# First attention: sums closed in four column groups, reciprocals widened by copies, one multiply

## The chip, the cores and the metric

The kernel runs on one core of one Trainium2 chip. A core has five engines that work side by side and wait for each other through semaphores: TensorE (PE in the profile, its weight loads PEld), VectorE (DVE), ScalarE (ACT), GpSimd (POOL) and SyncE (SP), which issues DMAs. The metric is the time of one execution on the device in microseconds, lower is better. The time before is 1979.07 us, the median of 3 runs (1977.02 to 1979.21).

## The reference

Four layers follow each other, each an attention and a feed-forward block on 2048 tokens of width 128. Only the first attention is touched. It has 16 query heads and 4 key heads of width 64, two sequences of 1024 tokens, and a causal mask:

```python
q = (x @ Wq + bq).reshape(b, s, NQ, D)
k = (x @ Wk + bk).reshape(b, s, NKV, D)
v = (x @ Wv + bv).reshape(b, s, NKV, D)
q = _rotary(q)
k = _rotary(k)
...
logits = jnp.einsum('bqhgd,bkhd->bhgqk', qg, k) * scale
logits = jnp.where(causal, logits, jnp.float32(-1e+30))
w = jax.nn.softmax(logits, axis=-1)
out = jnp.einsum('bhgqk,bkhd->bqhgd', w, v).reshape(b, s, NQ * D)
return out @ Wo + bo
```

The change concerns the division inside `softmax`: each weighted sum of values is divided by the sum of its row's exponentials.

## The kernel before

**Tiling.** An attention works through 16 head pairs (`j` in `attention_order`: 2 sequences times 8 pairs), and each pair through two chunks of 512 queries, c = 0 and c = 1. For a chunk, TensorE computes scores transposed, keys on the partitions and queries in the free dimension: one key tile of 128 keys, two heads, up to 512 queries each (`score`, written S below; 4 key tiles for c = 0 and 8 for c = 1). The two heads' scores go to PSUM banks P0 and P1, always these two, and ScalarE takes the exponentials from there into an SBUF tile `pr` (L1440, or L1435 for narrow tiles). The next S can only write P0 when the exponential has read it. GpSimd masks diagonal tiles (L1667) and adds the tiles up in `acc` (L1686, L1689). TensorE multiplies `pr` with the values (`pv`, written V), head 0 in PSUM partitions 0 to 63, head 1 in 64 to 127. Before the scores of a chunk, TensorE and VectorE find row maxima (`max`, written M; VectorE L2094, L2105) from other banks, TensorE transposes them (`rows`, written R, L993) and ScalarE negates them (L1418).

**Closing a chunk.** `close` (C) multiplies `acc` with a matrix of ones, which leaves the sum of exponentials of head 0 in partitions 0 to 63 of a bank and that of head 1 in 64 to 127, over 512 columns. Each such multiply is in fp32 and shows as two records, so that a close of the first attention is 4 records. ScalarE then makes a first reciprocal as exp(-ln(sum)) into `rd` (`yinv`, L1459 and L1461). VectorE improves it with one Newton step in two instructions (L2169, L2170) and multiplies the weighted values with it into `z` (L2176). These three are one item, `div` (D). After every second pair, `out` (O) multiplies `z` with the output weights (16 matmuls) and VectorE adds the result to `sacc`.

**What sets the order.** One list of items, made in `attention_order`, is walked by every engine's program; each engine issues its own instructions of each item in the order of the list and waits on semaphores. Nothing is reordered at run time. The string `STEPS[0]` spells the items of one pair: S, M, V, C, D, R, O as above, `q` and `k` projections for the next pair, `v` values, `+` one item of other work (layer norms, the router, its dispatch copies L1492 and GpSimd's gathers L1697). The digit of C, D and O is the distance back: C1, D1 close and divide the second chunk of the pair before (c = 1) while this pair begins, C0 and D0 the first chunk of this pair (c = 0) once its four tiles are added up. PSUM banks 4, 5, 6 and 2 rotate between close, projections, maxima, rows and out. The bank of a close is held from its item to its `div`.

The third attention (after 1430 us) already closes its chunks in four column groups of 32 columns, except the last pair, and takes another way for the reciprocal (a DMA to fold and to spread it). The second attention closes as the first.

## Time and profile before

| | |
|---|---|
| median of 3 runs | 1979.07 us |
| profiled execution | 1971.85 us, of which span 1970.1 us |
| PE busy | 1823.4 us, 93% of the span |
| DVE busy | 1348.2 us, 68% |
| POOL busy | 1203.3 us, 61% |
| ACT busy | 940.0 us, 48% |
| granted TensorE clock, mean | 0.975 |
| first attention | about 40 to 536 us |
| first feed-forward | about 536 to 657 us |

Busy is the union of the instructions' times on an engine. Matmuls overlap in the records, since one starts while the one before still drains, so what a matmul costs TensorE is better read from the distance between starts. The views used below are the page, the table of stretches (busy time of each engine between two times), the chain of waits (the work that ended last, followed back), the timeline of one engine and the groups of instructions by shape.

### The profile page before, as it was taken

How to read it: one execution, taken by the hardware profiler on the slowest of the kernel's cores; microseconds unless marked ns; L12 is line 12 of the kernel's file. 1: busy time of each engine (PE TensorE's matmuls, PEld its weight loads, DVE VectorE, ACT ScalarE, POOL GpSimd, SP SyncE). 2: the span in 40 equal slices, each digit the busy share in tenths (PEclk: the TensorE clock that was granted, in tenths of full speed). 3: DMA queues.
4: the chain of work that ended last, by engine and by line, in shares of the span. 5: the costliest groups of instructions: out<-in, count | busy, mean ns of one | idle time of the engine just before them, and what ended most of it. 6: DMA issues, size and time to landing. Idle time of an engine off the chain costs nothing.

```text
span 1970.1 us, 31876 instructions
## 1 busy us (share of the span) xinstructions
PE 1823.4 (93%) x10080; PEld 1264.4 (64%) x10080; DVE 1348.2 (68%) x3795; ACT 940.0 (48%) x1978; POOL 1203.3 (61%) x1424
## 2 busy tenths in 40 slices
PE   5999999999896799999999999999789999989985
PEld 4566666666595566766766667787556666655564
DVE  8888888888344867666666546547677787776633
ACT  2544445445455454555555434545334444444443
POOL 1766788889654457777777720011266676689853
PEclk8999999999998899999999999999889999999998
DMA  5224243232163433434434220000312223223243
GB/s 152 68 66 113 65 107 91 61 81 62 37 192 84 99 91 87 105 90 102 103 79 115 66 89 22 1 13 1 81 44 69 64 62 88 63 73 85 71 128 96
DMA packets 138568, 155.96 MB, mean 79 GB/s; under 512 B 34480, under 2 KB 78800, under 8 KB 138144
## 3 DMA queue, kind: packets, MB, share of 16 engines
q1 hardware_dynamic: 134304, 145.80, 30.3%
q0 software_dynamic: 4096, 8.12, 1.3%
q8 instruction: 81, 1.33, 0.3%
q14 instruction: 87, 0.71, 0.1%
HBM read 47.96 MB, written 17.52 MB: 33 GB/s over the span
## 4 chain that ended last, share of the span: by engine, by line
PE 59%; DVE 13%; POOL 11%; issue 6%; DMA 4%; ACT 3%; SPq 3%; POOLq 0%; DVEq 0%; ACTq 0%
PE P L894 58%; POOL acc L1689 4%; POOL yd L1706 3%; DVE P L2105 2%; DVE mx L2094 2%; POOL xg L1697 2%; SPq L1810 2%; DMA qA<-hq 1%; POOL acc L1686 1%; POOL pr L1667 1%; ACT pr L1440 1%; PE P L993 1%; DMA rb<-sum_share 1%; DVE mx L2115 1%; DVE mx L2105 0%
## 5 line engine op out<-in xcount | busy, mean ns | idle before, releaser
L1689 POOL TENSOR_TENSOR acc<-acc,pr 128x512 f32<-128x512 f32 (+5 forms) x640 | 659.3, 1049 | 42.8 <-ACT pr L1440 17.0
L1440 ACT ACTIVATE pr<-P 128x512 f32<-128x512 f32 (+1 forms) x768 | 396.4, 568 | 359.0 <-PE P L894 318.9
L894 PE MATMUL P<-pr,vt 128*64 128x512 f32 (+3 forms) x2304 | 403.2, 490 | 4.0 <-POOL pr L1667 4.0
L894 PE MATMUL P<-qA,kA 128*128 128x512 f32 (+2 forms) x1024 | 387.5, 382 | 9.5 <-ACT pr L1440 8.8
L894 PE MATMUL P<-qB,kB 128*128 128x512 f32 (+2 forms) x1024 | 366.2, 363 | 0.0
L894 PE MATMUL P<-kA,qA 128*128 128x512 f32 (+2 forms) x1152 | 314.6, 375 | 36.7 <-DMA qA<-hq 11.9
L1667 POOL TENSOR_SCALAR_AFFINE_SELECT pr<-pr 128x256 f32<-128x256 f32 x384 | 156.7, 409 | 314.1 <-ACT pr L1440 243.8
L894 PEld LDWEIGHTS P<-pr,vt 128*64 128x64 f32 x2304 | 154.5, 137 | 223.8 <-issue 190.3
L2094 DVE TENSOR_REDUCE mx<-P 128x1 f32<-128x512 f32 x384 | 243.1, 684 | 36.0 <-PE P L894 34.1
L894 PEld LDWEIGHTS P<-kA,qA 128*128 128x128 f32 x1152 | 192.1, 195 | 107.1 <-issue 25.2
L894 PEld LDWEIGHTS P<-qA,kA 128*128 128x128 f32 x1024 | 194.1, 190 | 85.8 <-ACT pr L1440 41.3
L1686 POOL TENSOR_TENSOR acc<-pr,pr 128x512 f32<-128x512 f32 (+3 forms) x160 | 213.5, 1343 | 58.2 <-ACT pr L1440 58.0
L2105 DVE CUSTOM_DVE_ANT_0 P<-P,maskQ 128x128 f32<-128x128 f32 (+3 forms) x384 | 177.7, 523 | 59.7 <-PE P L894 57.9
L894 PEld LDWEIGHTS P<-qB,kB 128*128 128x128 f32 x1024 | 194.3, 190 | 21.4
L2105 DVE CUSTOM_DVE_ANT_0 P<-P,maskQ,mx 128x384 f32<-128x384 f32 (+3 forms) x384 | 191.4, 556 | 16.6 <-PE P L894 15.2
L1435 ACT ACTIVATE pr<-P 128x512 f32<-128x512 f32 x192 | 86.9, 488 | 101.8 <-PE P L894 87.2
L2169 DVE SCALAR_TENSOR_TENSOR P<-P,rd 128x512 f32<-128x512 f32 x66 | 46.1, 698 | 122.4 <-ACT rd L1461 122.3
L894 PE MATMUL P<-xh,weights 128*128 128x512 f32 (+1 forms) x336 | 110.4, 411 | 5.9 <-DVE mx L2105 2.1
L1706 POOL DMA_INDIRECT yd<-y,ni x64 | 64.2, 1004 | 78.3 <-DVE y L2400 63.2
L2105 DVE DVE_READ_ACCUMULATOR2_ANT mx<- 128x1 f32 x768 | 109.9, 143 | 0.0
L894 PEld LDWEIGHTS P<-wo,z 128*128 128x128 f32 x768 | 93.4, 194 | 6.9 <-issue 3.1
L894 PE MATMUL P<-wo,z 128*128 128x128 f32 x768 | 96.2, 279 | 1.4 <-DVE z L2176 0.9
(354 smaller groups left out, 2696.6 us busy)
## 6 DMA issues: line engine op xcount, KB each, us to landing
qA<-hq SPq DMA_DIRECT2D x384, 128.0 KB, 2.4
kA<-stage SPq DMA_DIRECT2D x158, 128.0 KB, 2.4
qB<-qB SPq DMA_DIRECT2D x96, 128.0 KB, 2.3
kB<-stage SPq DMA_DIRECT2D x79, 128.0 KB, 2.4
rb<-sum_share SPq DMA_DIRECT2D x60, 128.0 KB, 2.9
yd<-in_c_zero SPq DMA_DIRECT2D x32, 128.0 KB, 2.7
w<-in_L_W SPq DMA_DIRECT2D x16, 256.0 KB, 5.0
xg<-xg SPq DMA_DIRECT2D x24, 129.0 KB
```

What stands on the lines that cost most here:

```text
L894: return P.matmul(out, lhs, rhs, start=start, stop=stop)
L1435: S.activation(a.pr[slot][:, :, 512 - wide:512], src, AF.Exp, scale=0.125).then_inc(s.free[b], 1)
L1440: S.activation(a.pr[slot][:, r, 512 - wide:512], m.bank[b][:, 512 - wide:512], AF.Exp, scale=0.125).then_inc(s.free[b], 1)
L1667: G.affine_select(tile, tile, [[0, 2], [1, 128]], ALU.is_ge, 0.0, 0, -1).then_inc(s.sel, 1)
L1686: G.tensor_tensor(acc[:, :, sl], p0[:, :, sl], pt[:, :, sl], ALU.add).then_inc(s.acc, 1)
L1689: G.tensor_tensor(acc[:, :, sl], acc[:, :, sl], pt[:, :, sl], ALU.add).then_inc(s.acc, 1)
L1697: G.indirect_dma_start(xgd[L], bass.IndirectOffsetOnAxis(ap=r.sidx[:, i // 2, i % 2:i % 2 + 1], axis=0), r.xs[i % 2][:], None).then_inc(s. ...
L1706: G.indirect_dma_start(yd[L], bass.IndirectOffsetOnAxis(ap=e.ni[u % 4][0:wide, t:t + 1], axis=0), e.y[u % 4][0:wide, t, :], None).then_inc ...
L1810: Y.dma_start(a.qA[slot][rows, r, :], hq[64 * r:64 * r + 64, :]).then_inc(s.q_dup[slot], 16)
L2094: V.reduce_max(mx[:, 8 + j:9 + j], ps[:, 0:wide], X).then_inc(s.free[b], 1)
L2105: top = V.tensor_tensor_reduce(tile, tile, m.maskQ[:, 512 - wide:512], 1.0, least, ALU.add, ALU.max, mx[:, j:j + 1])
L2169: chain(V.scalar_tensor_tensor(out=m.bank[b][:], in0=m.bank[b][:], scalar=-1.0, in1=y[:], op0=ALU.mult, op1=ALU.mult))
```

## The change

For the first attention only, a close becomes four multiplies with a ones matrix of 32 columns over 256 query columns each: partitions 0 to 31 hold head 0's queries 0 to 255, 32 to 63 head 0's queries 256 to 511, 64 to 95 and 96 to 127 the same of head 1. ScalarE's two instructions and VectorE's Newton step then run over 256 columns. `div` is split in three items:

- `newt` (N), VectorE: the Newton step over 256 columns; it frees the close's bank.
- `widen` (Y), ScalarE: eight copies of 32 partitions by 256 columns, from `rd` to `z`, two for each group, so that `z` holds the reciprocal in the layout of the weighted values.
- `div` (D), VectorE: one multiply of the weighted values with `z`, in place.

In `STEPS[0]` the sequence "C1 k0\" q1' q0\" D1 q1\" V1 k1 + S M2" becomes "C1 k0\" N1 q1' q0\" q1\" Y1 V1 k1 + S D1 M2", and "D0 R0 M6 S + M5 O0 M8 S" becomes "N0 R0 Y0 M6 S + M5 D0 M8 S O0". The wait of `yinv` for the division before it goes.

```diff
@@ -145,7 +145,7 @@
-                    self.held[b] = (HELD[kind],) + item[1:]
+                    self.held[b] = ("newt" if kind == "close" and item[1] == 0 else HELD[kind],) + item[1:]
@@ -191,6 +191,11 @@
+def quarters(L, b, p):
+
+    return L == 0 or not at_once(L, b, p)
@@ -201,10 +206,10 @@
-    0: ("k0 S q0 k0' R1 S q1 q0' S S C1 k0\" q1' q0\" D1 q1\" V1 k1 + S M2 S M0 k1' S v1 M4 + S M1 C0 V + k1\" + D0 R0 M6 S + M5 O0 M8 S v0 O1 M3 S S M7 V2 + + M9"),
+    0: ("k0 S q0 k0' R1 S q1 q0' S S C1 k0\" N1 q1' q0\" q1\" Y1 V1 k1 + S D1 M2 S M0 k1' S v1 M4 + S M1 C0 V + k1\" + N0 R0 Y0 M6 S + M5 D0 M8 S O0 v0 O1 M3 S S M7 V2 + + M9"),
@@ -1044,7 +1052,7 @@
-                if at_once(*k[0:3]):
+                if not quarters(*k[0:3]):
                     for r in range(2):
                         t = mm(ps[64 * r:64 * r + 64, :], m.ones[:], acc[:, r, :], True, True)
                 else:
...
@@ -1452,13 +1460,25 @@
-                own.mark(S.activation(a.rd[:], m.bank[b][:], AF.Ln))
+                cols = slice(0, 256 if quarters(L, bb, p) else 512)
+                own.mark(S.activation(a.rd[:, cols], m.bank[b][:, cols], AF.Ln))
                 own.settle()
-                S.activation(a.rd[:], a.rd[:], AF.Exp, scale=-1.0).then_inc(s.inv, 1)
+                S.activation(a.rd[:, cols], a.rd[:, cols], AF.Exp, scale=-1.0).then_inc(s.inv, 1)
+            elif kind == "widen":
+                a, old = m.A[k[0]], pl.put_out(*k)
+                z = a.z[pl.chunk(*k) % 4]
+                w.wait_ge(*pl.emptied("close", *k))
+                if old:
+                    w.wait_ge(*pl.filled("out", *old))
+                for g in range(4):
+                    for half in range(2):
+                        rows, cols = 64 * (g // 2) + 32 * half, 256 * (g % 2)
+                        t = S.copy(z[rows:rows + 32, cols:cols + 256], a.rd[32 * g:32 * g + 32, 0:256])
+                t.then_inc(s.widen, 1)
@@ -2161,19 +2181,41 @@
+            elif kind == "newt":
+                y = m.A[k[0]].rd[:, 0:256]
+                b, _, _ = od.bank[("close",) + k][0]
+                sums = m.bank[b][:, 0:256]
+                w.wait_ge(s.inv, od.nth("yinv", *k))
+                chain(V.scalar_tensor_tensor(out=sums, in0=sums, scalar=-1.0, in1=y, op0=ALU.mult, op1=ALU.mult))
+                V.scalar_tensor_tensor(out=y, in0=sums, scalar=2.0, in1=y, op0=ALU.add, op1=ALU.mult).then_inc(s.free[b], 1)
+            elif kind == "div" and k[0] == 0:
+                z = m.A[k[0]].z[pl.chunk(*k) % 4]
+                b, _, _ = od.bank[("pv",) + k + (0,)][0]
+                w.wait_ge(s.pv, od.nth("pv", *k, kts(k[0], k[3])[-1]))
+                w.wait_ge(s.widen, od.nth("widen", *k))
+                V.tensor_tensor(z[:], m.bank[b][:], z[:], ALU.mult).then_inc(s.free[b], 1)
...
```

How this moves instructions is shown at three places. First ScalarE's order around the close of a c = 0 chunk, one of the middle pairs, before. `rd` is the reciprocal, `mr` the negated maxima (R0), `xs` a dispatch copy, `pr` exponentials of scores.

```order
L1459 ACTIVATE rd_84<-P4 128x512
L1461 ACTIVATE rd_84<-rd_84 128x512
L1492 COPY xs0_41<-xf_2 128x128
L1418 ACTIVATE mr0_87<-P5 8x128
L1440 ACTIVATE pr2_49<-P0 128x512
L1440 ACTIVATE pr2_49<-P1 128x512
L1440 ACTIVATE pr3_50<-P0 128x384
L1440 ACTIVATE pr3_50<-P1 128x384
```

The same place now:

```order
L1468 ACTIVATE rd_84<-P4 128x256
L1470 ACTIVATE rd_84<-rd_84 128x256
L1512 COPY xs0_41<-xf_2 128x128
L1426 ACTIVATE mr0_87<-P5 8x128
L1480 COPY z2_82<-rd_84 32x256 x8
L1448 ACTIVATE pr2_49<-P0 128x512
L1448 ACTIVATE pr2_49<-P1 128x512
L1448 ACTIVATE pr3_50<-P0 128x384
L1448 ACTIVATE pr3_50<-P1 128x384
```

The eight copies stand behind the negation of the maxima and ahead of the exponentials of the next key tile.

Second ScalarE's order around the close of a c = 1 chunk (C1), before; `hq` is the upper half of the projected queries.

```order
L1459 ACTIVATE rd_84<-P5 128x512
L1461 ACTIVATE rd_84<-rd_84 128x512
L1384 CAST hq1_75<-P2 128x512
L1492 COPY xs0_41<-xf_2 128x128
L1440 ACTIVATE pr4_51<-P0 128x512
L1440 ACTIVATE pr4_51<-P1 128x512
```

And now:

```order
L1468 ACTIVATE rd_84<-P5 128x256
L1470 ACTIVATE rd_84<-rd_84 128x256
L1392 CAST hq1_75<-P2 128x512
L1480 COPY z3_83<-rd_84 32x256 x8
L1512 COPY xs0_41<-xf_2 128x128
L1448 ACTIVATE pr4_51<-P0 128x512
L1448 ACTIVATE pr4_51<-P1 128x512
```

Here the copies stand between the cast and the dispatch copy, again ahead of the exponentials.

Third TensorE's order behind a c = 0 close in a pair that ends with an output item, before. `kA` with `qA` into P2, P4, P5 or P6 are maxima, `qA,kA` and `qB,kB` into P0 and P1 are scores, `wo,z` is the output.

```order
L894 MATMUL P4<-kA_72,qA1_67 128x512
L894 MATMUL P5<-kA_72,qA1_67 128x512
L894 MATMUL P6<-wo_65,z0_80 128x128 x4
L894 MATMUL P6<-wo_65,z2_82 128x128 x4
L894 MATMUL P2<-kA_72,qA1_67 128x384
L894 MATMUL P4<-kA_72,qA1_67 128x384
L894 MATMUL P0<-qA2_68,kA_72 128x384
L894 MATMUL P0<-qB2_71,kB_73 128x384
L894 MATMUL P1<-qA2_68,kA_72 128x384
L894 MATMUL P1<-qB2_71,kB_73 128x384
```

And now:

```order
L902 MATMUL P4<-kA_72,qA1_67 128x512
L902 MATMUL P5<-kA_72,qA1_67 128x512
L902 MATMUL P6<-kA_72,qA1_67 128x384
L902 MATMUL P2<-kA_72,qA1_67 128x384
L902 MATMUL P0<-qA2_68,kA_72 128x384
L902 MATMUL P0<-qB2_71,kB_73 128x384
L902 MATMUL P1<-qA2_68,kA_72 128x384
L902 MATMUL P1<-qB2_71,kB_73 128x384
L902 MATMUL P4<-wo_65,z0_80 128x128 x4
L902 MATMUL P4<-wo_65,z2_82 128x128 x4
```

The output item moved behind the scores of the second key tile after the close. GpSimd's and SyncE's orders are unchanged.

## Rows read from the trace of the kernel before

**Rows 1.** The page: busy time of each engine, share of span, instructions.

```profile
PE 1823.4 (93%) x10080; PEld 1264.4 (64%) x10080; DVE 1348.2 (68%) x3795; ACT 940.0 (48%) x1978; POOL 1203.3 (61%) x1424
```

**Rows 2.** Stretches: start:end, length, busy of PE, PEld, DVE, ACT, POOL, clock, DMA.

```profile
60.00:250.00 190.00, 182.13 (x944) 117.63 (x940) 167.01 (x434) 88.02 (x184) 132.78 (x182) 0.99 0.32 77
250.00:500.00 250.00, 247.88 (x1303) 162.33 (x1303) 207.20 (x510) 126.24 (x270) 216.91 (x281) 1.00 0.32 77
```

**Rows 3.** The chain of waits between 300 and 388 us, by line.

```profile
by line: PE P L894 99.0%; PE P L993 1.3%
```

**Rows 4.** TensorE's timeline behind a c = 0 close: start, length, instruction.

```profile
370.10 1.08 PE L894 MATMUL P<-acc,ones 128*64 128x512 f32 x4
371.01 3.82 PE L894 MATMUL P<-pr,vt 128*64 128x128 f32 x20
374.77 0.30 PE L993 MATMUL P<-ident,mx 128*72 128x128 f32 x1
...
377.45 0.33 PE L894 MATMUL P<-qA,kA 128*128 128x384 f32 x1
```

**Rows 5.** TensorE's timeline around a close of the third attention.

```profile
1603.26 0.64 PE L894 MATMUL P<-acc,ones 128*32 128x256 f32 x8
1603.83 0.50 PE L894 MATMUL P<-qA,kA 128*128 128x512 f32 x1
```

**Rows 6.** ScalarE's timeline behind both closes: [idle before <- what ended it].

```profile
361.62 0.60 ACT L1459 ACTIVATE rd<-P 128x512 f32<-128x512 f32 x1 [0.30 <-PE P L894]
...
363.25 0.30 ACT L1492 COPY xs<-xf 128x128 f32<-128x128 f32 x1
364.94 1.09 ACT L1440 ACTIVATE pr<-P 128x512 f32<-128x512 f32 x2 [1.40 <-POOL acc L1689]
...
371.23 0.60 ACT L1459 ACTIVATE rd<-P 128x512 f32<-128x512 f32 x1 [0.70 <-PE P L894]
...
375.11 0.27 ACT L1418 ACTIVATE mr<-P 8x128 f32<-8x128 f32 x1 [2.43 <-PE P L993]
376.11 1.09 ACT L1440 ACTIVATE pr<-P 128x512 f32<-128x512 f32 x2 [0.74 <-PE P L894]
```

**Rows 7.** TensorE's timeline behind a c = 1 close.

```profile
360.49 1.08 PE L894 MATMUL P<-acc,ones 128*64 128x512 f32 x4
...
364.08 0.50 PE L894 MATMUL P<-qA,kA 128*128 128x512 f32 x1
...
366.17 0.42 PE L894 MATMUL P<-qA,kA 128*128 128x512 f32 x1
```

**Rows 8.** ScalarE's timeline: two copies of 32 partitions in a row.

```profile
97.32 0.36 ACT L1370 COPY m<-P 32x256 f32<-32x256 f32 x1 [5.28 <-PE P L894]
97.59 0.36 ACT L1371 COPY m<-P 32x256 f32<-32x256 f32 x1
```

**Rows 9.** Groups by shape: busy us, mean ns | idle before it and its releaser.

```profile
L1435 ACT ACTIVATE pr<-P 128x256 f32<-128x256 f32 x31 | 11.7, 378 | 0.0
L1333 ACT CAST rkh<-pr 128x256 fp32r<-128x256 f32 x1 | 0.4, 399 | 0.0
L2397 DVE TENSOR_TENSOR y<-P,b 128x256 f32<-128x256 f32 x24 | 10.1, 422 | 35.0 <-PE P L894 35.0
L2169 DVE SCALAR_TENSOR_TENSOR P<-P,rd 128x512 f32<-128x512 f32 x31 | 21.6, 697 | 31.4 <-ACT rd L1461 31.2
```

**Rows 10.** The chain of waits between 60 and 250 us, start and length.

```profile
126.40 0.61 DVE P L2169
...
227.46 0.62 DVE P L2169
```

**Rows 11.** The chain of waits behind a c = 1 close with new keys.

```profile
280.32 2.35 DMA qA<-hq
```

**Rows 12.** The last close of the first attention: TensorE, VectorE.

```profile
529.97 1.35 PE L894 MATMUL P<-acc,ones 128*64 128x512 f32 x4 [0.51 <-POOL acc L1689]
534.12 0.69 DVE L2176 TENSOR_TENSOR z<-P,rd 128x512 f32<-128x512 f32 x1
```

More of the change, by code:

```diff
@@ L308, in finish @@
                 od.add("out", *done)
+        elif kind in ("newt", "widen"):
+            if L == 0:
+                od.add(kind, *done)
         elif not at_once(L, b, p):
@@ L2168, in run @@
                 w.wait_ge(s.inv, od.nth("yinv", *k))
[L2169 to L2170 removed]
+                y, sums = (t[:, 0:256 if quarters(L, bb, p) else 512] for t in (y, m.bank[b]))
+                chain(V.scalar_tensor_tensor(out=sums, in0=sums, scalar=-1.0, in1=y, op0=ALU.mult, op1=ALU.mult))
+                V.scalar_tensor_tensor(out=y, in0=sums, scalar=2.0, in1=y, op0=ALU.add, op1=ALU.mult).then_inc(s.free[b], 1)
                 w.wait_ge(*pl.emptied("close", *k))
```

20 lines of the change are left out of this document (13 added, 7 removed).

## The prediction

> **What bounds the kernel now.** I read the page first: TensorE is busy 93% of the span, no other engine above 68% [rows 1]. Then the table of stretches, cut where the first attention changes its character. From 250 to 500 us TensorE is busy 247.9 of 250 us and ScalarE 126.2; from 60 to 250 us TensorE is busy 182.1 of 190 us and VectorE 167.0, because layer norms and the router run there too [rows 2]. The chain of waits settles the later stretch: from 300 to 388 us all of it is TensorE [rows 3]. So in the nine or ten later pairs every nanosecond taken from TensorE counts, and so does every wait put upon it. In the earlier six pairs VectorE shares the bound.
>
> A full stretch on TensorE does not say that ScalarE has room at every moment. Scores alternate between two banks, so that the next tile's scores wait for this tile's exponentials. That is why I go on to the timelines of both engines behind a close, and count from the close's first multiply.
>
> Behind a c = 0 close (370.10): values at 0.91, maxima transposed at 4.67, the second half of the second tile's scores at 7.35 [rows 4]. ScalarE: logarithm at 1.13, negated maxima at 5.01, exponentials of the first tile at 6.01 to 7.10 [rows 6]. Behind a c = 1 close (360.49): first tile's scores at 3.59, second half of the second tile's at 5.68 [rows 7], exponentials at 4.45 [rows 6].
>
> **TensorE's part.** A close costs 0.91 us now, from its first multiply to the next instruction [rows 4]. The third attention closes in the new form and shows 0.57 us (1603.83 - 1603.26) [rows 5]. That is 0.34 us less, and 32 closes make 10.9 us. It can be lost only where something else is late.
>
> **VectorE's part.** Three instructions of 0.70 us become two over 256 columns and one of 0.70. No Newton instruction of 256 columns is in the trace; an addition of that shape from PSUM takes 0.42 us [rows 9]. The Newton step then is about 0.87 us with the wait between its halves, so a chunk costs 1.57 instead of 2.10 us. The bounds of one Newton instruction are half of 0.70 and all of it, 0.35 and 0.70; I take 0.42, the nearest row.
>
> **ScalarE's part.** Logarithm and exponential shrink from 0.60 us [rows 6] or a little more each to about 0.38 [rows 9] and 0.40. Against it stand eight copies. A copy of 32 partitions and 256 columns from PSUM takes 0.36 us and the next starts 0.27 us after it (97.59 - 97.32) [rows 8]: fewer partitions save nothing, but successive instructions overlap by 0.09. From SBUF a cast of 256 columns takes 0.40 us [rows 9], so I take 0.31 from copy to copy, 2.48 us for eight. Ends: 0.27, as from PSUM, or 2.16; and 0.40 without overlap, or 3.20. In all ScalarE gets about 32 x (2.48 - 0.45) = 65 us more work. It has that much idle time, but the place decides.
>
> The Trainium skill has two rules on this place. "ScalarE: Activation LUTs", section "What ACT_TABLE_LOAD costs", gives 186 ns plus 0.833 ns per element and an overlap of about 93 ns between successive ones. By it a copy is 399 ns and the pitch 306, an estimate of 2.45 us for eight; the overlap agrees with rows 8. "VectorE: DVE Perf Modes", section on the TRN2 errata, speaks against the change: an SBUF source costs a fixed extra in every instruction, paid between instructions, so many small tiles pay it many times. By its table (224 cycles plus elements at 1.2 GHz) a copy is 400 ns and eight are 3.2 us, if none of it overlaps. Rows 8 show an overlap, though for a PSUM source; no row shows small copies from SBUF.
>
> **Behind a c = 0 close.** The copies are queued behind the negated maxima, which wait for TensorE's transpose behind all the values. So the 2.43 us in which ScalarE idles there [rows 6] don't cover them, although the Newton step is done long before. TensorE comes 0.34 earlier: negated maxima at 4.67 to 4.94, copies to 7.42, exponentials 7.42 to 8.51, and the second half of the second tile's scores at 8.56 (0.05 for the semaphore, as between close and logarithm) instead of 7.35. This is +1.21 us with the faster close counted. In pairs with an output item its 16 multiplies used to stand ahead of these scores and gave cover; now they stand behind, so the wait is the same. The same distance of 6.01 stands behind nine c = 0 closes from 252 to 488 us: 9 x 1.21 = 10.9 us.
>
> **Behind a c = 1 close.** Logarithm at 0.69 (the new close's records last 0.64 [rows 5], 0.05 for the semaphore), exponential to 1.49, Newton step to 2.40, copies 2.44 to 4.92, in about every second pair a dispatch copy (+0.20). Exponentials start at 4.92 or 5.12 instead of 4.45, and the second half of the next scores comes at 6.06 or 6.26 instead of 5.68: +0.48 on average. Seven later pairs show the 4.45: 3.4 us. In the two later pairs with new keys the chain goes from the reciprocal through the cast `hq` and its DMA of 2.35 us [rows 11]; the cast is ready some 0.9 us earlier and the copies are hidden: -1.8 us.
>
> **The first six pairs.** Here the c = 0 exponentials or the scores after them mostly wait for something else, and the copies are hidden. One pair pays in full and one a little (1.4), four c = 1 closes 0.4 each (1.6). Six closes elsewhere give 0.34 each (-2.0), and at five places the chain runs through VectorE's three instructions, as at 126.40 and 227.46 [rows 10], where about 0.5 each goes (-2.6). Sum -1.6 us.
>
> **The end of the attention.** Nothing hides the last chunk: from close to `z` it takes 534.12 + 0.69 - 529.97 = 4.84 us [rows 12]. New: logarithm at 1.05 (the close's 1.35 less 0.34, and the semaphore), 0.80 for both, Newton 0.91 with its wait, copies 2.6, multiply 0.73: 6.1. +1.3 us.
>
> **The multiply moved on VectorE** costs nothing by itself: its 0.7 us comes between maxima, just when TensorE is later by as much. Without that cover it would delay the next maxima by up to 0.7 us a pair. Nothing changes in GpSimd's or SyncE's order. GpSimd gets the masked tile behind a c = 0 close 1.4 us later (exponentials end at 8.51 instead of 7.10), but has 33 us of idle time in 250 to 500 us [rows 2], over 3 us a pair.
>
> **Sum.** 10.9 + 3.4 - 1.8 - 1.6 + 1.3 = +12.2 us. Against the profiled execution, 1971.85 us, that is 1984.1; it lies 7.2 below the median of the runs, so that I add the sum to the median: 1979.07 + 12.2 = 1991.3. With the pitch of 0.27 every one of some 21 places is 0.32 cheaper and the sum is +5.5 (1984.6); with 0.40 each is 0.72 dearer and it is +27.7 (2006.8). A measurement of this kernel tells about 0.2% from no change, here 4 us.
>
> **Rivals.**
>
> *Hidden copies (faster).* If ScalarE's copies are so much cheaper or the banks so much less tight that TensorE never waits, only the gains stand: -10.9, -2.6 from VectorE, and +1.3 at the end, or 1966.9. For it speak ScalarE's 50% of idle time and 2.43 us idle just there; against it, that this idle time ends with the instruction ahead of the copies, and that the exponential is followed at once by TensorE's use of its bank. It decides at 6.01 + 0.34 us behind a c = 0 close: there the copies may take 0.73 us at most. Chance 0.14.
>
> *Half hidden (no change).* The copies come every 0.27 us and VectorE's lighter load also takes waits of 0.2 to 0.3 us a pair from the later pairs: +5.5 - 4 = +1.5, 1980.6. For it speaks the pitch of rows 8, against it that the later pairs' chain has no VectorE in it [rows 3]. Chance 0.18.
>
> *Copies without overlap.* They read from SBUF and each pays its fixed part: 2006.8, as above. Against it stand rows 8. This is also what the errata rule of the Trainium skill would make of it. Chance 0.12.
>
> *The groups don't run side by side.* If the groups took turns, eight records at 0.91 / 4 would make a close 1.8 us, 32 x 1.25 us more than in the forecast: about 2031. Rows 5 speak against it. Chance 0.01.
>
> **Chances and range.** My forecast, copies that make TensorE wait at most places, has 0.55, with its own range 1984 to 2001. The range for 8 in 10 runs from 1974, into the half hidden case's spread, to 2006. Faster by over 0.2%: 0.17 (the hidden case and a tail of the next); within: 0.17; slower: 0.66.
>
> **What would show it.** Right: closes of 0.57 us; copies in a row of eight every 0.31 us, starting just after the negated maxima; exponentials 7.4 us behind a c = 0 close and 4.9 to 5.1 behind a c = 1 close; TensorE idle by more than 1 us before the scores there; the later pairs longer by some 1.7 us each; chain of waits with ScalarE's copies in it. Wrong: exponentials still at 6.0 less 0.34 behind a c = 0 close, copies inside the values' 3.8 us, or a time outside the range. If TensorE is idle but waits for VectorE's maxima, the moved multiply was the cost and not the copies.

## The result and the profile after

The changed kernel takes 2035.59 us (median of 3 runs, 2034.31 to 2037.71) against 1979.07 before: a ratio of 1.028, interval 1.0258 to 1.0302. It is 56.5 us slower, outside the predicted range of 1974 to 2006. The profiled executions lie 63.7 us apart in span (2033.8 against 1970.1), because that of before lies 7.2 below its median. All of the accounting below is between these two.

From the page after, the row of the engines and two groups:

```profile
PE 1837.5 (90%) x10208; PEld 1272.1 (63%) x10208; DVE 1334.0 (66%) x3795; ACT 1029.3 (51%) x2234; POOL 1201.7 (59%) x1424
...
L902 PE MATMUL P<-qA,kA 128*128 128x512 f32 (+2 forms) x1024 | 392.8, 387 | 59.2 <-ACT pr L1448 58.4
...
L1480 ACT COPY z<-rd 32x256 f32<-32x256 f32 x256 | 102.9, 402 | 14.3 <-DVE rd L2190 11.5
```

Compare [rows 1]: ScalarE has 89 us more work (1029.3 - 940.0), more than the predicted 65, and TensorE's share fell. The last number of the second row is the one to stop at: TensorE sat idle for 58.4 us ahead of scores, until ScalarE's exponentials had read the bank. The same group before:

```profile
L894 PE MATMUL P<-qA,kA 128*128 128x512 f32 (+2 forms) x1024 | 387.5, 382 | 9.5 <-ACT pr L1440 8.8
```

The stretches after, to be held against [rows 2], start:end, length, busy of PE, PEld, DVE, ACT, POOL, granted clock, DMA:

```profile
60.00:250.00 190.00, 168.38 (x900) 108.88 (x900) 147.10 (x401) 110.98 (x255) 118.33 (x158) 0.96 0.29 71
250.00:500.00 250.00, 226.33 (x1220) 147.66 (x1218) 176.55 (x452) 153.19 (x359) 193.90 (x259) 0.97 0.31 74
```

In 250 to 500 us TensorE went from 247.9 to 226.3 us busy, with fewer matmuls done, and the granted clock from 1.00 to 0.97. TensorE's waits in that stretch (us in total, times, longest), after:

```profile
PE P L902 <- ACT pr L1448: 22.0, 14, 2.0
PE P L902 <- DMA qA<-hq: 1.0, 3, 0.4
```

The first of these waits did not appear there before at all. The chain of waits between 300 and 388 us, nearly all TensorE before [rows 3], gives TensorE's matmuls 2.7% after and ScalarE's copies 6.9%. Its largest shares are "issue" (29.0%, time in which the profile shows no wait) and GpSimd's additions (24.5%), so the chain alone wouldn't have named the copies; the waits above and the timelines below do. Now the places of [rows 6] and [rows 4], in a middle pair. ScalarE's timeline behind a c = 0 close, after:

```profile
339.36 0.38 ACT L1468 ACTIVATE rd<-P 128x256 f32<-128x256 f32 x1 [0.28 <-PE P L902]
339.78 0.42 ACT L1470 ACTIVATE rd<-rd 128x256 f32<-128x256 f32 x1
...
343.37 0.27 ACT L1426 ACTIVATE mr<-P 8x128 f32<-8x128 f32 x1 [2.98 <-PE P L1001]
343.54 3.29 ACT L1480 COPY z<-rd 32x256 f32<-32x256 f32 x8
346.85 1.09 ACT L1448 ACTIVATE pr<-P 128x512 f32<-128x512 f32 x2
```

TensorE's timeline of the same stretch:

```profile
338.65 0.64 PE L902 MATMUL P<-acc,ones 128*32 128x256 f32 x8
339.22 3.87 PE L902 MATMUL P<-pr,vt 128*64 128x128 f32 x20
343.03 0.30 PE L1001 MATMUL P<-ident,mx 128*72 128x128 f32 x1
...
347.50 0.44 PE L902 MATMUL P<-qA,kA 128*128 128x384 f32 x1 [1.99 <-ACT pr L1448]
...
347.99 0.44 PE L902 MATMUL P<-qA,kA 128*128 128x384 f32 x1
...
348.44 3.17 PE L902 MATMUL P<-wo,z 128*128 128x128 f32 x16
```

The close costs 0.57 us, as forecast. The copies start 4.89 us behind it, just behind the negated maxima, as forecast. But eight of them take 3.29 us and not 2.48: one lasts 0.40, so that they start (3.29 - 0.40) / 7 = 0.413 us apart, with no overlap and a small gap. Exponentials start at 8.20 (forecast 7.42, before 6.01), and the second half of the second tile's scores starts at 9.34 (forecast 8.56, before 7.35).

The same behind a c = 1 close, ScalarE, beside the c = 1 rows of [rows 6]; its close started at 361.09:

```profile
361.81 0.39 ACT L1468 ACTIVATE rd<-P 128x256 f32<-128x256 f32 x1
362.23 0.42 ACT L1470 ACTIVATE rd<-rd 128x256 f32<-128x256 f32 x1
...
363.60 3.30 ACT L1480 COPY z<-rd 32x256 f32<-32x256 f32 x8 [0.48 <-DVE rd L2190]
366.93 1.09 ACT L1448 ACTIVATE pr<-P 128x512 f32<-128x512 f32 x2
```

Copies at 2.51 and exponentials at 5.84 behind the close, where 4.92 was forecast. The scores come at 7.06, or 7.26 with a dispatch copy, against 5.68 before [rows 7].

The last close, as [rows 12]: VectorE's multiply into `z` starts at 590.90, and this is 7.02 us from close to its end (forecast 6.1, before 4.84).

```profile
590.90 0.69 DVE L2196 TENSOR_TENSOR z<-P,z 128x512 f32<-128x512 f32 x1 [3.43 <-ACT z L1480]
```

One thing was in no step of the forecast. Three stretches around the wait above, same columns as the stretches before:

```profile
345.00:348.90 3.90, 1.91 (x12) 1.40 (x11) 3.09 (x7) 3.81 (x10) 0.80 (x2) 1.00 0.38 103
348.90:352.30 3.40, 3.40 (x17) 3.21 (x16) 0.65 (x2) 0.23 (x1) 3.23 (x4) 0.50 0.00 0
352.30:356.00 3.70, 3.70 (x20) 2.20 (x19) 2.99 (x13) 1.06 (x3) 3.53 (x6) 0.99 0.05 18
```

TensorE idled about 2 us, and soon after that its granted clock is at the lower of its two levels (1.2 instead of 2.4 GHz) for 3.4 us, while it is busy all the time. The 16 output multiplies at 348.44 take 3.17 us there; at half speed 3.4 us of work lose 1.7. In the next pair the wait is the same but no such stretch follows, and the 16 multiplies take 1.95 us, as in the kernel before. TensorE after, in that next pair:

```profile
380.95 0.44 PE L902 MATMUL P<-qA,kA 128*128 128x384 f32 x1 [1.98 <-ACT pr L1448]
...
381.89 1.95 PE L902 MATMUL P<-wo,z 128*128 128x128 f32 x16
```

From the first close to just behind the last there are ten such stretches after, and two before. Of 15 waits of 1.8 to 2.3 us behind c = 0 closes, nine have one at their end or up to 1.4 us later; the other six don't, and no run shows what tells them apart.

**Where the 63.7 us lie**, by closes:

| stretch | before | after | difference | forecast |
|---|---|---|---|---|
| start to first close | 59.3 | 60.8 | +1.5 | 0 |
| to the c = 0 close of the seventh pair ("first six pairs") | 193.2 | 210.6 | +17.4 | -1.6 |
| to the last close ("later pairs") | 277.5 | 313.2 | +35.7 | +12.5 |
| to the end | 1440.1 | 1449.2 | +9.1 | +1.3 |

The first row is no effect of the change: nothing in front of the first close differs, and of the kernels below two have the same 60.7 to 60.8 us and the others 59.3 to 59.4.

### The profile page after: what moved, and what is told of

Its sections match the earlier page's. It is cut to its first block, busy times and chain, and to the rows that moved or that the text cites. A ratio compares the mean times of both kernels' runs of the same rounds, so it can differ in the third digit from the quotient of the medians.

```text
span 2033.8 us, 32365 instructions
## 1 busy us (share of the span) xinstructions
PE 1837.5 (90%) x10208; PEld 1272.1 (63%) x10208; DVE 1334.0 (66%) x3795; ACT 1029.3 (51%) x2234; POOL 1201.7 (59%) x1424
## 4 chain that ended last, share of the span: by engine, by line
PE 47%; POOL 15%; DVE 14%; issue 11%; ACT 8%; DMA 3%; SPq 2%; POOLq 0%; DVEq 0%; ACTq 0%
PE P L902 46%; POOL acc L1709 7%; ACT z L1480 3%; POOL xg L1717 2%; DVE P L2125 2%; DVE mx L2114 2%; POOL acc L1706 2%; POOL pr L1687 2%; POOL yd L1726 2%; ACT pr L1448 1%; DMA qA<-hq 1%; SPq L1830 1%; DMA rb<-sum_share 1%; DVE mx L2135 1%; DVE mx L2125 0%
## 5 line engine op out<-in xcount | busy, mean ns | idle before, releaser
L902 PE MATMUL P<-qA,kA 128*128 128x512 f32 (+2 forms) x1024 | 392.8, 387 | 59.2 <-ACT pr L1448 58.4
L1687 POOL TENSOR_SCALAR_AFFINE_SELECT pr<-pr 128x256 f32<-128x256 f32 x384 | 157.4, 410 | 354.8 <-ACT pr L1448 285.8
L902 PE MATMUL P<-kA,qA 128*128 128x512 f32 (+2 forms) x1152 | 315.8, 378 | 35.5 <-DMA qA<-hq 12.2
L1706 POOL TENSOR_TENSOR acc<-pr,pr 128x512 f32<-128x512 f32 (+3 forms) x160 | 213.0, 1340 | 73.6 <-ACT pr L1448 73.6
L1480 ACT COPY z<-rd 32x256 f32<-32x256 f32 x256 | 102.9, 402 | 14.3 <-DVE rd L2190 11.5
L902 PE MATMUL P<-wo,z 128*128 128x128 f32 x768 | 104.9, 295 | 3.2 <-DVE z L2196 2.3
L902 PEld LDWEIGHTS P<-wo,z 128*128 128x128 f32 x768 | 102.6, 210 | 7.4 <-issue 2.8
```

The costliest lines, as they stand in the source:

```text
L902: return P.matmul(out, lhs, rhs, start=start, stop=stop)
L1480: t = S.copy(z[rows:rows + 32, cols:cols + 256], a.rd[32 * g:32 * g + 32, 0:256])
L1687: G.affine_select(tile, tile, [[0, 2], [1, 128]], ALU.is_ge, 0.0, 0, -1).then_inc(s.sel, 1)
L1706: G.tensor_tensor(acc[:, :, sl], p0[:, :, sl], pt[:, :, sl], ALU.add).then_inc(s.acc, 1)
```

## The experiments

Twelve kernels were run. A ratio stands to the kernel before, run on the same chip. My theory after the result: the copies cost by their place and their full 0.41 us each, and the half-clock stretches come from the waits that the copies cause. The rivals were the moved order, the new close itself (it might lower the clock), VectorE's two steps, and the SBUF source.

| kernel | median us (before) | ratio, interval | first six | later | behind |
|---|---|---|---|---|---|
| changed kernel | 2035.6 (1979.1) | 1.028, 1.0258 to 1.0302 | 210.6 | 313.2 | 1449.2 |
| no copies | 1961.8 (1978.3) | 0.9927, 0.9901 to 0.9954 | 183.3 | 272.4 | 1444.1 |
| four copies | 1968.6 (1978.3) | 0.9951, 0.9938 to 0.9965 | 186.4 | 276.9 | 1448.2 |
| copies ahead of maxima | 2005.5 (1978.3) | 1.0147, 1.0117 to 1.0177 | 208.8 | 285.8 | 1450.2 |
| copies from PSUM | 2030.8 (1978.3) | 1.0281, 1.0253 to 1.031 | 213.0 | 305.1 | 1447.7 |
| by destination | 2031.7 (1975.1) | 1.0286, 1.0267 to 1.0304 | 214.5 | 313.0 | 1446.7 |
| filler matmuls | 2020.0 (1975.1) | 1.0233, 1.0213 to 1.0252 | 205.2 | 306.7 | 1445.1 |
| half on VectorE | 1985.7 (1975.1) | 1.005, 1.0031 to 1.0069 | 193.1 | 286.9 | 1446.5 |
| parts 5, 1, 1, 1 | 1994.7 (1977.7) | 1.0098, 1.0079 to 1.0117 | 204.4 | 283.1 | 1444.8 |
| parts 4, 1, 1, 2 | 2001.6 (1977.7) | 1.0134, 1.0113 to 1.0155 | 206.8 | 286.5 | 1443.1 |
| 5, 1, 1, 1, new order | 1987.1 (1982.7) | 1.0018, 1.0005 to 1.003 | 197.9 | 274.6 | 1448.9 |
| 6, 1, 1, new order | 1990.1 (1982.7) | 1.0036, 1.0021 to 1.005 | 201.8 | 277.5 | 1448.5 |
| early copies behind | 1983.2 (1976.8) | 1.0031, 1.0019 to 1.0044 | 199.4 | 274.5 | 1448.3 |

The last three columns are the stretches of the profiled execution, cut as above.

**No copies.** The eight copies are left out, and VectorE multiplies with the reciprocals as they lie, so that the queries are divided by each other's sums. Since VectorE now reads `rd`, ScalarE's logarithm waits for the multiply before it again.

```diff
-                for g in range(4):
-                    for half in range(2):
...
-                        t = S.copy(z[rows:rows + 32, cols:cols + 256], a.rd[32 * g:32 * g + 32, 0:256])
-                V.tensor_tensor(z[:], m.bank[b][:], z[:], ALU.mult)
+                V.tensor_tensor(z[:]..., m.bank[b][:]..., m.A[0].rd[:, 0:256].unsqueeze(1).broadcast_to([128, 2, 256]), ALU.mult)
```

> The changed kernel with the eight widening copies left out: VectorE multiplies straight with the 256 reciprocals, read twice, which is the wrong layout, so the division isn't computed; everything else, the new close, the half-width reciprocal and the new order of the list, stays. Theory (the copies hold up the exponentials on ScalarE, TensorE waits for its score banks, and the clock dips that follow come from those waits): without copies 1964 to 1972 us, no idle time of TensorE behind a c = 0 close, and the 3.4 us stretches at half clock in the first attention gone. Rival A (the moved output item and the moved multiply cost it): 1990 us or more. Rival B (the dips of the clock come from the four-group close itself): the waits go but the dips stay, about 1980 to 1985 us.

ScalarE's timeline behind a c = 0 close that started at 330.37, without copies:

```profile
335.08 0.27 ACT L1426 ACTIVATE mr<-P 8x128 f32<-8x128 f32 x1 [2.98 <-PE P L1001]
336.08 1.09 ACT L1448 ACTIVATE pr<-P 128x512 f32<-128x512 f32 x2 [0.73 <-PE P L902]
```

Exponentials at 5.72, second half of the scores at 7.07, and the stretch from 60 to 500 us shows TensorE 432.54 of 440 us busy at full clock:

```profile
60.00:500.00 440.00, 432.54 (x2418) 281.53 (x2418) 359.02 (x957) 208.31 (x469) 362.39 (x483) 1.00 0.33 79
```

The time, 1961.8, is 2 us below the expected range. So neither the order nor the new close costs anything on balance: with both in place and the copies gone the kernel beats the one before by 0.7%. Between the two ratios lie 0.0353 x 1978 = 70 us, the price of the copies with all that follows from them.

**Four copies** of 64 partitions; the layout that they make is not the one needed, so the division isn't the right one.

```diff
-                    for half in range(2):
-                        rows, cols = 64 * (g // 2) + 32 * half, 256 * (g % 2)
-                        t = S.copy(z[rows:rows + 32, cols:cols + 256], a.rd[32 * g:32 * g + 32, 0:256])
+                    rows, cols = slice(64 * (g // 2), 64 * (g // 2) + 64), 256 * (g % 2)
+                    t = S.copy(z[rows, cols:cols + 256], a.rd[rows, 0:256])
```

> Four copies of 64 partitions by 256 columns in place of eight of 32 (each pair of 32-partition halves in one instruction; z is then filled in the wrong layout, so the division isn't computed). Theory (0.416 us per copy instruction, whatever its partitions): copies take 1.7 us, exponentials behind a c = 0 close start at 6.6 us and behind a c = 1 close at 4.2, so 1970 to 1982 us. If the cost went by bytes or partitions, the four would take as long as the eight and the time would stay near 2035. Rival A (order): 1995 us or more.

The four start 2.51, 2.82, 3.23 and 3.54 us behind a c = 1 close: 0.31 apart where source and destination lie in the same partitions as those of the copy before, 0.41 where they change. The exponentials come at 4.16, as with none: four copies are hidden there. Behind c = 0 they come at 6.33 (expected 6.6), and the time of 1968.6 lies just below the expected range, since two of the three distances are not the 0.416 us of the expectation. No half-clock stretch falls between 60 and 520 us.

**Copies ahead of the maxima.** Behind a c = 0 close ScalarE copies first.

```diff
-... V + k1\" + N0 R0 Y0 M6 S + M5 D0 ...
+... V + k1\" + N0 Y0 R0 M6 S + M5 D0 ...
```

> All eight copies, but those of a c = 0 chunk stand ahead of the negated maxima in the list (N0 Y0 R0 in place of N0 R0 Y0), so they can run while TensorE multiplies the values. Theory: copies from 2.5 to 5.8 us behind a c = 0 close, exponentials at 6.1 instead of 8.2, as in the kernel before; the c = 1 closes still cost 1.4 to 1.6 us each: 1995 to 2008 us. Rival (the sum of ScalarE's extra work counts, not its place): 2025 to 2036 us.

ScalarE behind a c = 0 close that started at 299.55:

```profile
302.06 3.31 ACT L1480 COPY z<-rd 32x256 f32<-32x256 f32 x8 [0.78 <-DVE rd L2190]
305.39 0.27 ACT L1426 ACTIVATE mr<-P 8x128 f32<-8x128 f32 x1
305.56 1.05 ACT L1448 ACTIVATE pr<-P 128x512 f32<-128x512 f32 x2
```

The wait for TensorE's transpose now covers the copies: exponentials at 6.01 instead of 8.20, and the time is in the expected range. The later pairs take 27 us less. The first six take only 1.8 less: there the Newton step itself is late in four of the six (4.2 to 6.0 us behind the close, against 1.6 in the later pairs).

**Copies from PSUM.** VectorE leaves the refined reciprocal in the close's bank and ScalarE copies from there; the bank stays held until the last copy has read it.

```diff
-                V.scalar_tensor_tensor(out=y, in0=sums, scalar=2.0, in1=y, op0=ALU.add, op1=ALU.mult)
+                V.scalar_tensor_tensor(out=sums, in0=sums, scalar=2.0, in1=y, op0=ALU.add, op1=ALU.mult)
...
-                        t = S.copy(z[rows:rows + 32, cols:cols + 256], a.rd[32 * g:32 * g + 32, 0:256])
+                        t = S.copy(z[rows:rows + 32, cols:cols + 256], m.bank[b][32 * g:32 * g + 32, 0:256])
```

> The Newton step writes its result into the close's PSUM bank instead of rd, and the eight copies read it from there; the bank is held until they are done. Theory (an SBUF source is what keeps successive copies from overlapping; two copies of 32 partitions from PSUM started 0.27 us apart in the kernel before): a pitch of 0.27, exponentials at 7.1 us behind a c = 0 close and at 4.7 to 4.9 behind a c = 1 close, 1988 to 2004 us. Rival (0.416 us is the price of any such copy in a row of eight, or of one that starts in another partition than it reads): pitch and time stay, 2030 to 2040 us.

**By destination.** The same eight copies, those into the same 32 partitions behind each other.

```diff
-                for g in range(4):
-                    for half in range(2):
-                        rows, cols = 64 * (g // 2) + 32 * half, 256 * (g % 2)
+                for quad in range(4):
+                    for g in (2 * (quad // 2), 2 * (quad // 2) + 1):
+                        rows, cols = 32 * quad, 256 * (g % 2)
```

> The changed kernel with its eight copies in another order: the two that write the same 32 partitions of z follow each other, where before the two that read the same 32 partitions did. Theory (two successive copies overlap by 0.1 us only if they write the same partitions; in the run with four copies the starts alternated between 0.31 and 0.41 us apart): starts alternate 0.31 and 0.41, the exponentials start 0.4 us earlier behind each close, and some 30 places of 0.4 give 2020 to 2026 us. Rival (both source and destination have to stay in the same partitions): every pitch stays 0.41 and the time within 2030 to 2040 us.

The eight copies behind a c = 0 close, first read from PSUM, then ordered by destination:

```profile
342.24 2.97 ACT L1481 COPY z<-P 32x256 f32<-32x256 f32 x8
```

```profile
346.02 3.29 ACT L1480 COPY z<-rd 32x256 f32<-32x256 f32 x8
```

From PSUM one takes 0.36 us as in [rows 8], but they start (2.97 - 0.36) / 7 = 0.373 apart and not 0.27: there is no overlap either. The exponentials come earlier for it, at 7.88 us behind a c = 0 close. That this hardly shows in the time has a cause of its own: TensorE's maxima now wait for the bank that the copies read. TensorE's waits from 250 to 500 us, copies from PSUM:

```profile
PE P L902 <- ACT z L1481: 12.9, 7, 1.8
PE P L902 <- ACT pr L1448: 8.1, 6, 1.5
```

So this kernel tells how far apart the copies start, where its theory fell, and its time says little on what they cost, though it lies in the rival's range. By destination nothing moves, in the distances or in the time (2031.7), as that expectation's rival had it. In the changed kernel sources repeat from copy to copy and destinations change; in this one destinations repeat and sources change. The pairs that do overlap are those of the four-copy kernel and [rows 8], whose code copies twice from partitions 0 to 31 of a bank into partitions 0 to 31. All four observations fit one reading: a copy overlaps the one before when source and destination both stay in the same partitions. The overlapping copies from SBUF have 64 partitions, so that for 32 partitions the reading rests on [rows 8], from PSUM, alone. A widening has no two such copies.

**Filler matmuls.** Behind the c = 0 closes of 15 pairs six multiplies without use go ahead of TensorE's wait; nothing else is changed.

```diff
+IDLE.update({("max", 0, j // 8, j % 8, 1, 0, 2, 1): 6 for j in range(1, 16)})
```

> The changed kernel with six filler multiplies (identity by identity, as the kernel uses elsewhere) ahead of the maxima at which TensorE then waits for its score bank behind a c = 0 close, in 15 of 16 pairs; about 1.9 us of multiplies into 2.0 us of waiting. Theory (the 3.4 us stretches at half clock follow these waits, and each costs about 1.7 us): eight or more of the ten stretches go and the time falls to 2015 to 2025 us, though the copies take as long as before. Rival (the waits alone are the whole cost, the clock is read off wrongly): 2034 to 2042 us.

```profile
60.00:540.00 480.00, 446.75 (x2541) 292.45 (x2542) 358.80 (x950) 294.81 (x685) 350.48 (x464) 1.00 0.30 71
```

The clock is 1.00 up to 540 us, exponentials and scores stand at 8.20 and 9.34 as in the changed kernel, and from the first to the last close it takes 511.9 instead of 523.8 us. So the clock's share is about 12 us of trace, and by the ratios (1.028 less 1.0233) x 1978 = 9 us. It is an effect of the waits, not of the close, which shows no such stretch without copies. The time is in the range of the expectation's theory.

**Half on VectorE**, with the whole division: four of the eight copies go to VectorE, and ScalarE's four stand ahead of the maxima.

```diff
...
+                for quad in (2, 3):
+                    for g in (2 * (quad // 2), 2 * (quad // 2) + 1):
+                        rows, cols = 32 * quad, 256 * (g % 2)
+                        t = V.tensor_copy(z[rows:rows + 32, cols:cols + 256], m.A[0].rd[32 * g:32 * g + 32, 0:256])
...
```

> The division is complete. Four of the eight copies run on ScalarE and the other four on VectorE, each pair of copies to the same partitions in a row, and the c = 0 copies stand ahead of the negated maxima (N0 Y0 R0). Theory (four copies on ScalarE end before the exponentials are due at both closes, as the run with four copies showed for c = 1, and VectorE has 2.5 us of idle time behind a c = 0 close): exponentials at 5.7 and 4.2 us, no half-clock stretches in the first attention, 1962 to 1972 us. Rival (VectorE is the bound of the first six pairs, and its copies delay the maxima everywhere): 1972 to 1985 us.

In the later pairs exponentials mostly come at 5.72 and 4.19 to 4.40, as expected, but the time is above the theory's range and 0.7 us above that of the rival, whose late maxima are what the trace shows. VectorE and TensorE behind a c = 0 close that started at 376.38:

```profile
378.88 3.99 DVE L2201 COPY z<-rd 32x256 f32<-32x256 f32 x4
```

```profile
383.65 0.45 PE L902 MATMUL P<-kA,qA 128*128 128x384 f32 x1 [0.74 <-DVE mx L2116]
```

Of VectorE's 128 copies the median took 0.307 us but the longest 3.367, so that four take 3.99 and the maxima behind them keep TensorE waiting. GpSimd in the same stretch:

```profile
377.91 3.73 POOL L1711 TENSOR_TENSOR acc<-acc,pr 128x512 f32<-128x512 f32 x3
```

The first VectorE copy lasts from 378.88 to 381.78 and ends 0.14 us behind the last of these additions. All 12 copies of over 1 us do the same: each starts while GpSimd adds tiles and ends some 0.15 us behind the end of an addition. That the additions hold the copies is what this suggests; no run took them away.

**Parts.** All eight stay on ScalarE, with the whole division, but some go behind the exponentials of the next tiles, where ScalarE idles 0.42 us each. Behind c = 0 seven stand ahead of the maxima and one behind the next tile.

```diff
+PARTS = {1: (5, 1, 1, 1), 0: (7, 1)}
...
-... + S D1 M2 S M0 k1' S v1 M4 + S M1 C0 V + k1\" + N0 R0 Y0 M6 S + M5 D0 ...
+... + S Y1 M2 S Y1 M0 k1' S Y1 D1 v1 M4 + S M1 C0 V + k1\" + N0 Y0 R0 M6 S Y0 + M5 D0 ...
```

> All eight copies stay on ScalarE, but they are issued in parts. Behind a c = 1 close five come ahead of the next exponentials and one behind each of the next three score tiles, ahead of the multiply; behind a c = 0 close seven come ahead of the negated maxima and one behind the next tile's exponentials. Theory (the copies cost only where they delay the first exponentials of a tile, and the half-clock stretches come from TensorE's waits that follow): behind c = 1 the first exponentials 4.1 to 4.7 us behind the close (5.84 in the changed kernel, 4.16 without copies), behind c = 0 5.7 to 6.1 us (8.20 changed, 5.72 without copies), second half of the scores 6.7 to 7.3 us; no or nearly no half-clock stretch between 60 and 500 us; time 1964 to 1974 us, ratio 0.992 to 0.999 to the kernel before. Rival (every copy costs its 0.41 us wherever it stands, since the exponentials and not the copies alone pace the pair): exponentials later by the same sum over a pair, 32 x about 2 us less than in the changed kernel is not regained, time 2000 us or more. Rival (the late multiply holds the bank of the weighted values and delays them): first exponentials as in the theory but the weighted values wait for VectorE's multiply, 1975 to 1990 us.

> As the kernel with parts 5, 1, 1, 1, but behind a c = 1 close four copies ahead of the next exponentials, one behind each of the next two tiles and two behind the third. Theory: first exponentials behind c = 1 at 4.1 to 4.3 us, the gap with two copies is 0.83 us, which ScalarE has idle there; time 1963 to 1973 us, within 2 us of the kernel with 5, 1, 1, 1. Rival (two copies in one gap delay the fourth tile's exponentials): 0.2 to 0.4 us for each of 16 pairs, so 3 to 6 us above the kernel with 5, 1, 1, 1.

With 5, 1, 1, 1 exponentials stand about where the theory had them in most later pairs (5.72 behind c = 0, 4.60 to 4.81 behind c = 1), yet neither kernel came near its time. VectorE and TensorE of the kernel with 5, 1, 1, 1, behind the c = 1 close at 373.57:

```profile
383.05 0.69 DVE L2205 TENSOR_TENSOR z<-P,z 128x512 f32<-128x512 f32 x1 [0.95 <-ACT z L1489]
383.66 1.28 DVE L2123 TENSOR_REDUCE mx<-P 128x1 f32<-128x512 f32 x2
```

```profile
384.49 0.64 PE L908 MATMUL P<-acc,ones 128*32 128x256 f32 x8 [0.83 <-POOL acc L1718]
```

The multiply waits 0.95 us for the last copy, the maxima stand in the queue behind it, and the next close starts just after the first of them, 0.83 us late. The profile names GpSimd as the releaser, but this close needs only additions that were long done (by 378.4), and its bank, P4, is read last by the first of those two maxima, which ends about 384.3: a releaser named wrongly. With 4, 1, 1, 2 the multiply and the fourth tile's exponentials come 0.36 us later still in every second later pair and 0.4 in those with new keys, and the later pairs are 3.4 us longer. That is what its own rival named, though the time grew by 7 us and not by 3 to 6; the intervals of the two ratios overlap a little.

**New order.** D1 behind M4, the Newton step ahead of the second piece of router work, the dispatch copy ahead of the copies; once with 5, 1, 1, 1 and once with 6, 1, 1. The lines are set against the kernel with parts 5, 1, 1, 1 above.

```diff
-... q1\" Y1 V1 k1 + S Y1 M2 S Y1 M0 k1' S Y1 D1 v1 M4 + S M1 C0 V + k1\" + N0 Y0 R0 ...
+... q1\" V1 k1 + Y1 S Y1 M2 S Y1 M0 k1' S Y1 v1 M4 D1 + S M1 C0 V + k1\" N0 + Y0 R0 ...
```

> The kernel with parts 5, 1, 1, 1 lost its gain in two places that its trace shows: VectorE's multiply stands in its queue ahead of the maxima of M4 and waits 0.95 us for the last copy, so that the bank for the next close comes free 0.83 us late; and in the first six pairs the seven copies wait for a Newton step that stands behind the router's search for the largest values on VectorE, and hold up the negated maxima behind them (exponentials at 8.6 us behind a c = 0 close against 5.72 without copies). Here D1 stands behind M4, the Newton step ahead of the router's second piece, and the dispatch copy ahead of the copies. Theory (VectorE's order is what was left): no wait of TensorE for the maxima ahead of a c = 0 close, 9.8 to 10.2 us from a c = 1 close to it (10.92 before this change of order, 9.33 to 9.7 without copies), exponentials behind c = 1 at 4.6 us, behind c = 0 at 5.7 to 6.1 us in the first pairs too; last close 520 to 532 us; time 1966 to 1982 us. Rival (the copies on ScalarE themselves set the pace by delaying GpSimd's additions): last close stays above 540 us, time 1988 us or more.

> As the kernel before in this call, but behind a c = 1 close six copies ahead of the exponentials and two behind the next two tiles, so that the multiply never waits. Theory: the sixth copy costs 0.41 us in the exponentials behind each c = 1 close (5.0 us), so 16 x 0.41 = 6.6 us more than with 5, 1, 1, 1: 1972 to 1989 us. Rival (VectorE's late multiply still costs with 5, 1, 1, 1): equal or faster than 5, 1, 1, 1.

From a c = 1 close to the c = 0 close behind it most later pairs now take 9.83 us, as expected, and are 274.6 us long, 2.9 less than before the change. The sixth copy puts the exponentials behind c = 1 off by 0.41 us, as the theory had it, but the time grows by 3 us and not by 6.6: the later pairs by 2.9, and the two ratios' intervals overlap. The last close comes at 533.21, 1.2 us past the expected end, and the time is 5 us above the range: the first six pairs stay at 197.9 us, 4.7 more than before, where the c = 0 copies still start 2.6 to 7.9 us behind the close. Four of them start at 4.6 to 6.8 us and wait for the Newton step behind VectorE's other work; those at 7.9 stand in ScalarE's queue behind copies for the router. TensorE waits 10.5 us in these pairs for the negated maxima that stand behind the copies.

**Early copies behind.** As 5, 1, 1, 1 in the new order, but in the first six pairs the c = 0 copies stand behind the first exponentials.

```diff
+        if L == 0 and j < 6:
+            steps = steps.replace("Y0 R0 M6 S Y0", "R0 M6 S Y0 Y0")
```

> As the kernel with parts 5, 1, 1, 1 and VectorE's new order, but in the first six pairs the copies of the c = 0 chunk stand behind the negated maxima and the first exponentials behind them, not ahead. In the kernel before this change these copies waited up to 7 us behind the close for the Newton step, which stands behind the router's work on VectorE, and held the negated maxima and the exponentials back (exponentials at 7.7, 8.4 and 9.9 us behind the close in the second half of these pairs); without copies these come at 5.7 us, and the second tile's scores only at about 7 to 10 us. Theory (in the first six pairs the cost is that ScalarE stands behind VectorE's Newton step): exponentials behind their c = 0 closes at 5.7 us as without copies, from the first close to the first c = 0 close of pair 6 about 188 to 193 us (197.9 with the copies ahead, 183.3 without copies, 193.2 in the kernel before the change), time 5 to 10 us less than with the copies ahead, 1976 to 1983 us where the kernel before takes 1979 to 1983. Rival (VectorE's router work sets these pairs by itself): exponentials earlier, but the second tile's scores and the next closes no earlier, time within 3 us of the kernel with the copies ahead.

ScalarE and VectorE in the third pair, close at 125.40:

```profile
131.11 1.09 ACT L1457 ACTIVATE pr<-P 128x512 f32<-128x512 f32 x2 [0.73 <-PE P L911]
132.08 3.30 ACT L1492 COPY z<-rd 32x256 f32<-32x256 f32 x8
```

```profile
135.49 0.69 DVE L2208 TENSOR_TENSOR z<-P,z 128x512 f32<-128x512 f32 x1 [1.26 <-ACT z L1492]
```

Exponentials at 5.71 as expected, but these pairs take 199.4 us, not 188 to 193. Now VectorE's multiply waits 1.26 us for the copies (1.3 to 2.3 in all six pairs), and VectorE shares the bound there. The ratio, 1.0031, is not below the 1.0018 of the kernel with the copies ahead. My theory of these pairs falls, and its rival holds: moving the copies out of ScalarE's way only moves the wait.

No kernel that does the whole division beat the one before. The best ratio is 1.0018.

## Why the prediction was wrong

**Right.** TensorE's close at 0.57 us. VectorE's Newton step of 0.43 and 0.42 us. The place of the copies, behind the negated maxima at 4.9 and behind the Newton step at 2.5. The two pairs with new keys, where they are hidden, though the gain there is 0.3 us in the offsets of the scores and not 1.8. The multiply moved on VectorE and the output item moved on TensorE, which cost nothing on balance, as the kernel without copies shows. The sign, and the mechanism of exponentials that hold a bank.

**The step that failed** is the one in ScalarE's part: "successive instructions overlap by 0.09 ... so I take 0.31 from copy to copy, 2.48 us for eight". They start 0.413 apart, 3.3 us for eight, above the upper end of 0.40 that I had kept. The overlap of [rows 8] was a property of that pair of copies and not of ScalarE: it needs the partitions to stay the same, and the copies of a widening cannot keep them. The Trainium skill ("ScalarE: Activation LUTs", "What ACT_TABLE_LOAD costs") gives the overlap without this condition, and here the measurement decides. Its other rule ("VectorE: DVE Perf Modes", TRN2 errata), a fixed extra for an SBUF source in every instruction, agrees with 0.40 against 0.36 us from PSUM, but the lost overlap is the larger part and is lost from PSUM too. Priced by the prediction's own rule, 21 places at 0.82 us more are +17 us, so that the sum would have been +29 and not +12. That is 2008.5, still 27 us short of the measured time: two more terms failed, the clock, put at nothing, and the first six pairs, put at -1.6. Of the 51.5 us between forecast and profiled difference (63.7 - 12.2), the waits of the later pairs hold 14, the clock there 9, the first six pairs 19, the end 8 and the start 1.5.

In the later pairs that accounts for what the offsets show. Nine c = 0 places lose 1.9 to 2.0 us each (forecast 1.21), 17.6 in all, counting 1.71 us for the output item where it moved behind the scores (379.50 - 377.79 in the trace of before). Seven c = 1 places lose 1.26 to 1.58 (forecast 0.48), 10.2. The last pair and the pairs with new keys gain 1.2. That is 26.6 of the 35.7 us; the remaining 9 are about what five half-clock stretches of up to 1.7 us cost. The output item before, TensorE, and what follows it:

```profile
377.79 1.95 PE L894 MATMUL P<-wo,z 128*128 128x128 f32 x16
379.50 0.70 PE L894 MATMUL P<-kA,qA 128*128 128x512 f32 x2
```

**Terms that were missing.** The clock: I let TensorE idle 1.2 us at some places and charged only the wait. With waits of 2 us the clock fell behind nine of fifteen of them, and the filler kernel puts this at 9 to 12 us over the attention. The chance of it was in no rival.

**The first six pairs** were not hidden (+17.4 instead of -1.6). The step read exponentials that wait for something else as room for copies. There it overlooked that the copies wait for the Newton step, which stands behind the router's work on VectorE, so that a wait of the reciprocal became a wait of the exponentials. And in the fourth pair, where the Newton step is early, the copies stand behind the negated maxima as in the later pairs, and the exponentials start at 8.20 as there. The third pair after, c = 0 close at 131.04, VectorE and ScalarE:

```profile
135.22 0.41 DVE L2189 SCALAR_TENSOR_TENSOR P<-P,rd 128x256 f32<-128x256 f32 x1
135.66 0.42 DVE L2190 SCALAR_TENSOR_TENSOR rd<-P,rd 128x256 f32<-128x256 f32 x1
```

```profile
135.75 0.27 ACT L1426 ACTIVATE mr<-P 8x128 f32<-8x128 f32 x1 [3.17 <-PE P L1001]
136.12 3.30 ACT L1480 COPY z<-rd 32x256 f32<-32x256 f32 x8
```

Before the change nothing on ScalarE waited for this Newton step; now the exponentials do. In this pair the Newton step puts the copies off by 0.2 us only (5.08 behind the close against 4.88), in the fifth by 1.3 and in the first and sixth by 1.9 and 2.0. How the +17.4 us divide between this wait and the rest is open: with the exponentials freed of it, in the last kernel above, the pairs still took 6.2 us more than before. The twelve places there lose 11.2 us in the offsets of the second tile's scores, or 16.3 with the output item counted at three of them; four half-clock stretches after against one before have a part in it.

**The end.** From the last close to `z` +2.2 instead of +1.3. Of these 0.9 us more, 0.7 are once more the copies; the close itself fell into a half-clock stretch. Some 7 us more behind it are not explained by the change: all the other kernels' profiled executions are 3 to 10 us longer there than this one of before, the one without copies too. This stays open, and the medians, 56.5 us apart, have less of it.

**The rivals.** The copies without overlap (2006.8, chance 0.12) had the right mechanism and lie 29 us too low, since they were priced with the same hidden first pairs and without the clock. (By the prediction's own terms, 21 x 0.72, the sum is +27.3 and the time 2006.4. In the hidden case the mark for the exponentials has to be 6.01 less 0.34, as the signs of being wrong have it, and not 6.01 + 0.34: without copies they came at 5.72.) Had I weighed the two ends of the copy by the partitions in the code and not by which row was nearest in shape, that case would have led.

## What to carry to other kernels

Work put in front of an instruction that frees a bank costs its whole length, however idle its engine is on average, unless the engine waits at just that place for something else; and it takes on every wait that it brings along. When a duration is taken from a row, ask whether the row's distance to its neighbour depends on where the two operands lie, and keep the case without overlap as the base. Where a full TensorE gets waits of about 2 us, price the clock behind them too, as here it fell behind nine of fifteen, and try the version without the added work first: here one run showed that the kernel gains 0.7% if the copies cost nothing at all.

## What the runs showed that I had not expected

In these runs ScalarE's copies of 256 columns overlap by 0.09 us only when source and destination both stay in the partitions of the copy before (0.31 against 0.41 from SBUF, 0.27 against 0.37 from PSUM). VectorE's copies of 32 by 256 took 0.307 us in the median and up to 3.367, and each of the long ones ended just behind one of GpSimd's additions. The granted clock of a TensorE that is otherwise full fell to one half for 3.4 us behind nine of fifteen waits of about 2 us, and behind none of those in which six multiplies stood.
